# Six shared tiles behind the routed ones instead of five, and the first products of layer 1 moved ahead of the border between the phases

## What is computed

```
# layer 0
xn = layernorm(x)
x = x + attention(xn) + ffn0(xn)
# ffn0: softmax router, top 2 of 8 experts, and one shared expert for every token
#   expert(x) = silu((x @ w1 + b1) * (x @ w3 + b3)) @ w2 + b2          (256 -> 352 -> 256)
# layer 1
xn = layernorm(x)
z = sigmoid(xn @ Wz + bz);  h~ = xn @ Wh + bh
h_t = (1 - z_t) * h_(t-1) + z_t * h~_t;   attn1 = sigmoid(h @ Wg + bg) * h
# ffn1: s = sigmoid(xn @ gate.T); the better group of 4 experts, its top 2, weights normalised
#   lat = xn @ fc1.T; routed = sum_e weight_e * relu2(lat @ w1_e) @ w2_e; then @ fc2.T
#   shared = relu2(xn @ up.T) @ down.T
x = x + attn1 + ffn1(xn)
```

## Time and profile before

| | |
|---|---|
| runs | 1211.9, 1207.92, 1206.44 us |
| median | 1207.92 us |
| span of the profiled execution | 1206.9 us (the page gives no other time of it) |
| PE busy | 1111.1 us, 92% |
| DVE, ACT, POOL busy | 897.4, 676.1, 529.1 us |
| first product of the experts phase | 462.10 us |
| first product of layer 1 | 829.58 us |

### The profile page before, as it was taken

The page is one execution under the profiler, slowest core; times in us unless marked ns, Lnnn a source line. Parts: engine busy times, 40 slices in busy tenths (PEclk is TensorE's granted clock), DMA queues, the critical chain, the costliest instruction groups (busy, mean ns, idle before and its releaser), DMA issues. The chain is left out here.

```text
span 1206.9 us, 26712 instructions
## 1 busy us (share of the span) xinstructions
PE 1111.1 (92%) x8873; PEld 745.7 (62%) x8905; DVE 897.4 (74%) x2217; ACT 676.1 (56%) x1463; POOL 529.1 (44%) x743
## 2 busy tenths in 40 slices
PE   4789999999999987998999999996999999999998
PEld 2345555555455546887999888983656646546555
DVE  5778887888888757975766657775876877877876
ACT  2256565555556564565656656664654664664653
POOL 5443434334243235844444444423646547447414
PEclk9689999999999999999999999998999999999999
DMA  5538544354533404665232453452241331331211
GB/s 146 112 67 237 102 80 98 80 111 96 93 81 80 99 19 155 215 179 165 79 127 83 119 163 124 126 149 85 89 141 36 106 126 48 105 102 64 96 45 62
DMA packets 105044, 129.36 MB, mean 107 GB/s; under 512 B 14976, under 2 KB 92736, under 8 KB 103936
## 3 DMA queue, kind: packets, MB, share of 16 engines
q1 hardware_dynamic: 93952, 109.27, 33.8%
q0 software_dynamic: 6912, 18.88, 5.6%
q10 hardware_dynamic: 4096, 0.14, 0.2%
HBM read 84.70 MB, written 43.38 MB: 106 GB/s over the span
## 5 line engine op out<-in xcount | busy, mean ns | idle before, releaser
L537 ACT ACTIVATE p<-bank 128x384 f32<-128x384 f32 (+1 forms) x384 | 191.9, 530 | 186.4 <-PE bank L937 118.8
L757 DVE TENSOR_REDUCE neg_max<-bank 128x1 f16<-128x384 f32 (+3 forms) x352 | 219.7, 640 | 64.7 <-PE bank L925 56.4
L452 POOL TENSOR_SCALAR_AFFINE_SELECT p<-p 128x256 f32<-128x256 f32 x256 | 104.1, 410 | 247.3 <-ACT p L537 246.7
L922 PE MATMUL bank<-k_stack,q_stack 96*128 96x384 f16 (+3 forms) x512 | 133.5, 313 | 20.1 <-DVE neg_max L757 13.1
L1377 POOL DMA_INDIRECT fetched<-xn_dram,token_now x80 | 81.2, 1015 | 42.8 <-POOL token_now L1373 30.6
L937 PE MATMUL bank<-q_stack,k_stack 97*128 97x512 f16 (+1 forms) x256 | 91.5, 362 | 6.0 <-ACT p L537 3.5
L2006 POOL TENSOR_TENSOR up_lo<-up_sq,up_hi 128x512 f16<-128x512 f32 x32 | 43.9, 1399 | 120.7 <-ACT up_hi L2063 120.7
L2017 POOL TENSOR_TENSOR he_lo<-he_sq,he_hi 128x512 f16<-128x512 f32 x64 | 79.9, 1268 | 36.7 <-ACT he_hi L2106 36.6
L1461 ACT ACTIVATE a<-xbank,b 128x256 f32<-128x256 f32 (+1 forms) x126 | 58.6, 468 | 51.2 <-PE xbank L149 47.8
L1549 DVE TENSOR_TENSOR h_lo<-h,h_hi 128x256 f16<-128x256 f32 x159 | 68.4, 433 | 24.4 <-ACT h_hi L1470 23.5
L955 PE MATMUL bank<-p,v_aug 128*32 128x512 f32 (+3 forms) x1024 | 83.5, 445 | 0.8 <-DVE o_rows L737 0.8
(11 more groups left out here) (342 smaller groups left out, 3375.2 us busy)
## 6 DMA issues: line engine op xcount, KB each, us to landing
w_bc<-wT_dram SPq DMA_DIRECT2D x8, 2048.0 KB, 8.0
y_routed_dram<-y SPq DMA_DIRECT2D x37, 256.0 KB
w<-in_w SPq DMA_DIRECT2D x10, 704.0 KB, 6.9
pack<-in_pack SPq DMA_DIRECT2D x12, 342.0 KB, 4.1
xr<-in_x SPq DMA_DIRECT2D x8, 512.0 KB, 7.3
xn_dram<-xn SPq DMA_DIRECT2D x8, 512.0 KB, 3.1
qk_hi_dram<-qk_hi SPq DMA_DIRECT2D x16, 256.0 KB, 2.4
qk_lo_dram<-qk_lo SPq DMA_DIRECT2D x16, 256.0 KB, 2.4
```

Source lines behind the costliest of these rows:

```text
L452: pool.affine_select(out=diagonal, in_=diagonal, pattern=[[0, 2], [1, P]], compare_op=ALU.is_ge, fill=0.0, base=0, channel_multiplier=-1). ...
L537: act.activation(p32[:, s // GH % 2, s % GH, cols], s_bank[n][:, 0:cols.stop - cols.start], ACT.Exp).then_inc(p_exp.sem, 1)
L757: dve.tensor_reduce(neg_max[:, g % 2, 0:GH * TT].rearrange("p (h t) -> p h t", t=TT)[:, heads[0]:heads[-1] + 1, j], a_bank[c % 2][:, 0:len ...
L922: pe.matmul(to[:, at * w:(at + 1) * w], q_stack[0:STK, u, h0 + h, j * P:(j + 1) * P], k_stack[0:STK, u, h0 + h, 0:w], start=at == 0, stop= ...
```

## The change

The tail has six tiles and the head ten. The normalising of the first rows moves to stage 4, behind `hidden`; their turning stays in the last stage, now 5, as do the two halves, which leave the tail functions. `first_slots(1)` and `neg_bz` go to stage 4. In its tail PE appends `first_products`: `gate`, `lat` and `z0` of step 0; ACT makes the sigmoid and `lat_hi` there. Step 0 of layer 1 starts with the wait before `h0`. SP loads the three bias tensors in the prologue of the experts phase. The PSUM banks are declared once, and `l1_y` shares the memory of `turned`.

```diff
-TAIL_TILES = 5
+TAIL_TILES = 6
...
                 if stage not in (HEAD, TURN):
-                    if stage == 1:
-                        load_turned(HEAD_TILES + 3, HEAD_TILES + 4, i)
+                    if stage in range(1, TAIL_TILES - 3):
+                        load_turned(HEAD_TILES + 2 + stage, HEAD_TILES + 3 + stage, i)
...
# SP, prologue of the experts phase (were at the start of layer 1's block)
+                sp.dma_start(front.bias[:, :], w["bias"]).then_inc(front.loaded.sem, 16)
+                sp.dma_start(front.corr[:, :], w["corr"].partition_broadcast(P)).then_inc(front.loaded.sem, 16)
+                sp.dma_start(front.neg_bz[:, :], w["bias"][:, BZ:BZ + DC]).then_inc(front.loaded.sem, 16)
...
# ACT, tile
-                if stage == TAIL_TILES - 1:
-                    first_normalise()
                 for m in range(HM):
                     hidden(i, m)
+                if stage == TAIL_TILES - 2:
+                    first_normalise()
+                if stage == TAIL_TILES - 1:
+                    first_x_high()
...
             def tail(i, u):
+                act.wait_ge(front.lg_psum.sem, front.lg_psum.at(0))
+                act.activation(front.sc[:, :, :], bank[0][:, 0:TT * E].rearrange("p (t e) -> p t e", e=E),
+                               ACT.Sigmoid).then_inc(front.sc_s.sem, 1)
+                act.wait_ge(front.lat_psum.sem, front.lat_psum.at(0))
+                act.activation(front.lat_hi[:, :], bank[1][:, :], ACT.Copy).then_inc(front.lat_hi_s.sem, 1)
...
# DVE, tile
-                elif stage == TAIL_TILES - 3:
+                elif stage == TAIL_TILES - 4:
                     first_sums(0)
                     first_sums(1)
-                elif stage == TAIL_TILES - 2:
+                elif stage == TAIL_TILES - 3:
                     first_sums(2)
                     first_sums(3)
                     first_statistics()
+                elif stage == TAIL_TILES - 2:
+                    dve.wait_ge(front.loaded.sem, front.loaded.at(0))
+                    dve.tensor_scalar(front.neg_bz[:, :], front.neg_bz[:, :], -1.0, None, ALU.mult).then_inc(front.neg_bz_s.sem, 1)
+                    first_slots(1)
+                elif stage == TAIL_TILES - 1:
+                    first_x_low()
...
# PE
+            def tail(i, u):
+                out(i, u)
+                first_products(i)
+
+            def first_products(i):
+                pe.wait_ge(front.xT_lo_s.sem, front.xT_lo_s.at(0))
+                pe.wait_ge(prod_s.sem, prod_s.at(i))
...
+                for t in range(TT):
+                    tok = slice(t * P, (t + 1) * P)
+                    mm = three_products(pe, bank[0][:, t * E:(t + 1) * E], ...)
+                mm.then_inc(front.lg_psum.sem, 1)
+                from_x(bank[1][:, :], "fc1", LAT).then_inc(front.lat_psum.sem, 1)
+                from_x(bank[2][:, :], "wz", P).then_inc(front.z_psum.sem, 1)
...
# layer 1, PE's step (ACT's sigmoid and lat_hi likewise)
-                pe.wait_ge(xT_lo_s.sem, xT_lo_s.at(b))
                 if before:
+                    pe.wait_ge(xT_lo_s.sem, xT_lo_s.at(b))
                     pe.wait_ge(he_sq_s.sem, he_sq_s.at(b - 1))
...
+                    mm.then_inc(lg_psum.sem, 1)
+                    from_x(ring("lat")[:, :], "fc1", slice(0, LAT)).then_inc(lat_psum.sem, 1)
+                    from_x(ring("z0")[:, :], "wz", slice(0, P)).then_inc(z_psum.sem, 1)
                 pe.wait_ge(sc_s.sem, sc_s.at(b))
```

More of the change, by code:

```diff
@@ L102, in sb @@
             return ctx.enter_context(nc.sbuf_tensor(name, shape, dt))
+        self.bank = [ctx.enter_context(nc.psum_tensor(f"bank{i}", [P, 512], F32)) for i in range(8)]
         self.xr = sb("xr", [P, TT, D])
+        self.x1 = sb("x1", [P, TT, D])
         self.x_loaded = Signal(nc, ctx, "x_loaded", 16)
@@ L223, in mix_phase @@
         run = route["run"]
-        bank = [ps(f"bank{i}", [P, 512]) for i in range(8)]
+        bank = carried.bank
         w_loaded = sig("w_loaded", 16 * 8)
@@ L1114, in __init__ @@
         self.tile_out = sb("y", [P, ETOK // P, D])
+        self.bias = sb("l1_bias", [P, 3 * DC])
+        self.neg_bz = sb("neg_bz", [P, DC])
+        self.corr = sb("corr", [P, E])
+        self.sc = sb("l1_sc", [P, TT, E])
+        self.lat_hi = sb("lat_hi", [P, S], F16)
         self.slot_s = sig("slot_s", 2)
@@ L1126, in __init__ @@
         self.tile_stored = sig("y_stored", 16)
+        self.loaded = sig("l1_loaded", 16 * 3)
+        self.neg_bz_s = sig("neg_bz_s", 1)
+        self.lg_psum = sig("l1_lg_psum", 1)
+        self.lat_psum = sig("lat_psum", 1)
+        self.z_psum = sig("z_psum", DC)
+        self.sc_s = sig("sc_s", 1)
+        self.lat_hi_s = sig("lat_hi_s", 1)
 def experts_phase(nc, w, dram, consts, route, packed, front, carried):
@@ L1181, in experts_phase @@
         posf = sb("posf", [P, T // P, 2])
-        bank = [ctx.enter_context(nc.psum_tensor(f"xbank{i}", [P, 512], F32)) for i in range(8)]
+        bank = carried.bank
         front_bank = bank[6:8]
@@ L1501, in first_normalise, with first_x_high @@
                 ins.then_inc(front.xn_ready.sem, 1)
-            def tail(i, u):
+            def first_x_high():
                 for c in range(DC):
@@ L1636, in first_statistics, with first_x_low @@
                 ins.then_inc(front.dve_ln.sem, 2)
-            def tail(i, u):
+            def first_x_low():
                 for c in range(DC):
@@ L1642, in tail @@
                                       ALU.subtract).then_inc(front.xT_lo_s.sem, 1)
-                total_shared(i, TAIL_TILES - 1, (HEAD_TILES - 1) // 2)
-                first_slots(1)
+            def tail(i, u):
+                total_shared(i, HEAD_TILES + TAIL_TILES - 2)
             def done(n, ins):
@@ L1779, in after_first, with tail, from_x @@
                     pe.nop(nofuse=True)
-            over_experts(pe, lambda: None, new_expert, tile, after_first, lambda e, u, first: None, table, out)
+            def tail(i, u):
+                out(i, u)
[3 more added lines that the diff above has]
+                pe.wait_ge(prod_s.sem, prod_s.at(i))
+                def from_x(to, name, n):
+                    at, (_, width) = PACK[name]
+                    return three_products(pe, to, lambda c: pack_hi[:, at + c * width:at + c * width + n],
+                                          lambda c: pack_lo[:, at + c * width:at + c * width + n],
+                                          lambda c: front.xT_hi[:, c, :], lambda c: front.xT_lo[:, c, :], range(DC))
+                at = PACK["gate"][0]
+                for t in range(TT):
+                    tok = slice(t * P, (t + 1) * P)
+                    mm = three_products(pe, bank[0][:, t * E:(t + 1) * E], lambda c: front.xT_hi[:, c, tok],
+                                        lambda c: front.xT_lo[:, c, tok], lambda c: pack_hi[:, at + c * E:at + (c + 1) * E],
+                                        lambda c: pack_lo[:, at + c * E:at + (c + 1) * E], range(DC))
+                mm.then_inc(front.lg_psum.sem, 1)
+                from_x(bank[1][:, :], "fc1", LAT).then_inc(front.lat_psum.sem, 1)
+                from_x(bank[2][:, :], "wz", P).then_inc(front.z_psum.sem, 1)
+            over_experts(pe, lambda: None, new_expert, tile, after_first, lambda e, u, first: None, table, tail)
 PACK = {}
@@ L1816, in layer1_phase @@
         NU = UP // P
-        bias = sb("l1_bias", [P, 3 * DC])
-        neg_bz = sb("neg_bz", [P, DC])
-        corr = sb("corr", [P, E])
+        bias, neg_bz, corr, sc, lat_hi = front.bias, front.neg_bz, front.corr, front.sc, front.lat_hi
         minus_half, nothing, minus_mean, shift = front.minus_half, front.nothing, front.minus_mean, front.shift
@@ L1855, in layer1_phase @@
         comb_hi, comb_lo = (sb(f"comb_{k}", [P, S], F16) for k in ("hi", "lo"))
-        y = sb("l1_y", [P, TT, D])
-        bank = [ctx.enter_context(nc.psum_tensor(f"ybank{i}", [P, 512], F32)) for i in range(8)]
+        y = carried.turned[:, :, :, :, :].rearrange("p a b c n -> p (a b c n)").bitcast(F32)[:, 0:TT * D].rearrange("p (t d) -> p t d", t=TT)
+        bank = carried.bank
         out_bank, comb_bank = (bank[3], bank[4], bank[5], bank[7]), bank[6]
@@ L2022, in _ @@
         def _(act):
-            act.wait_ge(loaded.sem, loaded.at(0))
-            act.wait_ge(neg_bz_s.sem, 1)
+            act.wait_ge(front.neg_bz_s.sem, 1)
             def normalise(b, u):
@@ L2065, in step @@
             def step(b, u, before, more):
[L2066 to L2070, removed]
+                if before:
+                    act.wait_ge(lg_psum.sem, lg_psum.at(b))
+                    act.activation(sc[:, :, :], ring("gate")[:, 0:TT * E].rearrange("p (t e) -> p t e", e=E),
+                                   ACT.Sigmoid).then_inc(sc_s.sem, 1)
+                    act.wait_ge(lat_psum.sem, lat_psum.at(b))
+                    act.activation(lat_hi[:, :], ring("lat")[:, :], ACT.Copy).then_inc(lat_hi_s.sem, 1)
```

(10 more changed lines are left out.)

32 lines of the change are left out of this document (9 added, 23 removed).

## The result

The changed kernel takes 1211.83 us (median of 5 runs, 1210.75 to 1215.3) against 1207.14 us before in the same runs (1205.88 to 1211.9): a ratio of 1.0037 with a 95% interval of 1.0022 to 1.0052, or +4.5 us (2.7 to 6.3). The forecast was +5.0 us and 1212.9 us. The profiled execution took 1210.75 us, the fastest of its five, with a span of 1209.0, 2.1 more than the span before. That is why the spans differ by less than the medians.

A forecast was written before the change was run, and what follows sets the result against it. PE, busy 92% of the span, was taken to set the end, except at step 0, where the gathers do. Head -1.4, tail and border +2.4, clock +4.0 made +5.0 on 1207.92: 1212.9 us, range 1205 to 1217.5.

The forecast's parts named there:

- Head: Table after tile 7: PE idles 5.4 us for DVE's place(7), so one tile less saves only 1.4 us; clock 2.0.
- Tail: Last tiles before the border: the sixth tile fills the wait for the normalised rows and costs only +0.2 us.
- First products ahead of the border: Tail's end into step 0: gate, lat and z0 delay border and gathers; u3 2.4 us later, including the tail's +0.2.
- The gathers end the chain: Step 0 of layer 1: POOL's eighth gather ends last, so PE idles 5.3 us before u3.
- third rival: Step 0: gathers do not set it, PE's h0 starts 2.5 us earlier; sum -1.9, 1206.0 us; chance 0.10.
- Clock: Behind the waits before the table and before u3: half clock costs 2.0 us each, +4.0 for both.
- first rival: Both new waits of PE: the clock stays up; sum +1.0, 1208.9 us; chance 0.17.
- second rival: Both new waits of PE: clock stays low long after, 3.3 us each; sum +7.6, 1215.5 us; chance 0.22.

The follow-up runs named there:

- e5: The kernel before with only its table one tile earlier, waiting for prod of tile 7: 1213.76 us, ratio 1.0042 to the kernel before.
- e9: The changed kernel with the table's products reordered, the eight columns of place(7) multiplied last: 1204.4 us, ratio 0.9969 to the kernel before.
- e2: The changed kernel with gate, lat, z0 and ACT's sigmoid and lat_hi back behind the border: 1208.23 us, ratio 1.0016 to the kernel before.
- e8: The changed kernel with DVE's sums of step 0 put behind its first squares and scans: 1206.79 us, ratio 0.9990 to the kernel before.
- e12: e10 with gate, lat, z0 and the sigmoid back behind the border: 1201.59 us, ratio 0.9951 to the kernel before.
- e10: The changed kernel with the edits of e8 and e9 together: 1202.45 us, ratio 0.9948 to the kernel before.
- e4: The changed kernel with unread products filling PE's waits before the table and before u3: 1207.86 us, ratio 0.9999 to the kernel before.
- e1: The changed kernel with POOL's eight gathers issued ahead of the border instead of behind it: 1211.61 us, ratio 1.0032 to the kernel before.
- e11: The changed kernel with POOL waiting for ACT's early sigmoid, then one small memset before the border: 1216.86 us (2 runs), ratio 1.0076 to the kernel before.
- e3: The changed kernel with the last eight columns of in_column placed by POOL instead of DVE: 1209.17 us, ratio 1.0011 to the kernel before.

## Why the prediction was right

In the profiled pair the head gives +0.5 us, the routed tiles -1.1, tail and border up to u3 +1.45, the clock from u3 to g0 +1.3: together the 2.1 by which the spans differ. I take the -1.1 as no part of the change (the last statistics start at 815.73 instead of 816.31, and a wait of DVE for a stored `y`, 1.19 us in the trace of before, is not in the other), though no run isolates it; without it the trace gives +3.2, inside the interval of 2.7 to 6.3. By steps:

- **Head, -1.4 + 2.0 = +0.6 forecast.** +0.5 seen in this pair. The wait came as written (4.96 against 5.4 us, from DVE's last columns), and e5 and e9 show it from both sides: put in alone it costs 5 us, filled it gives 5.4 back. The table's half clock was 2.35, not 2.0, and it is no constant: behind waits of 4.9 to 5.1 us the table lost 1.2 (e5), 2.35 (after) and 2.7 us (e2).
- **Tail, +0.2.** The tile did fill the wait. DVE's sum was the last thing before `out(5)`, as forecast. With the statistics 0.58 us earlier in this execution, its start at 824.70 stands for 825.28, where I had 825.95; its end, 826.83, stands for 827.41 against `out(4)`'s 827.77. So the term was -0.4. Of the difference to my +0.2, 0.4 us arise already at DVE's first `prod` of stage 4, which starts 0.29 us behind the start of the last statistics (816.02 against 815.73); before it was 0.70 (817.01 against 816.31).
- **First products ahead of the border, +2.4 with the tail.** They end 3.2 us behind `out(5)`, the block opens 0.34 behind PE where I took 0.6, and u3 starts 1.45 us later than in the kernel before (845.15 + 0.58 less 844.28). So this step was about 1 us too high: 0.6 from the tail's term, the rest from the products and the opening. The mechanism is e2's: 2.1 per mille, 2.5 us, back when they are moved behind the border again (2.4 at g0 in its trace).
- **The gathers end the chain.** True by the chain of waits, and by e8: take DVE's sums out of the way and the wait before u3 is gone. The third rival priced PE's early start at 2.5 us; with the gathers off the path, e12 against e10 has 0.6 us of it at g0.
- **Clock, +4.0.** 2.35 + 1.28 = 3.6 in the trace of e4, 4.6 us by its ratio, within its uncertainty. In step 0 PE itself lost more: its wait before g0 shrank from 0.82 to 0.27 us, which gave 0.55 back. The first rival (clock stays up) had +1.0; the second needed 3.3 at each place. Neither was the case here. (Read off the low stretch is rather 6.8 us than 6.6, 821.2 to 828.1; half of it is 3.4.)
- **Forecast +5.0, measured +4.5.** The mechanisms were right as far as the runs show them; that the numbers lie only 0.5 us apart is in part luck. Taken from the traces, the terms come to 0.5 + 1.45 + 1.3 = 3.2 us, so the sum was some 1.8 us too high, 1.0 at the border and 0.7 in the clock of step 0, and the ratio with its interval of 2.7 to 6.3 can't tell 3.2 from 5.0.

The page "TensorE: Matmul & The Clock Gate" of the Trainium skill (section Terms) prices a throttled stretch by its length times the share of pulses withheld. The trace agrees once the length is counted only where PE works. The granted clock was low from 517.8 (0.89 in 517 to 518, 0.50 in 518 to 519) to 524.6 (0.69 in 524 to 525), 6.8 us. From 519.54, the table's first product, to 524.6 are 5.1 of them, of which half is 2.5, and 2.35 were lost. The 1.8 us before that, in which PE was idle, cost nothing, which is why the second rival's 3.3 was too much.

## What to carry to other kernels

A tile moved into a wait saves only what is not given back elsewhere: here the 6 us of the head went into a longer wait ahead of the table (4.96 us instead of 0.76) and a table at the half clock (2.35), and a later border (1.45 us in the trace) with the low clock behind u3 (1.3) came on top. Before moving work over a border, find what ends last behind it: moving one step of DVE, which stood between the gathers and PE, gave 5.7 us, where moving products back over the border (e2) gave 2.5 and moving gathers ahead of it (e1) nothing clear. Where a wait stays, let PE do in it what is ready, as 56 of the table's 64 column products in e9.

## What the runs showed of the hardware

- **Behind POOL's last instruction a block took long to end.** From there to the opening of the next block 8.2 us (e1, gathers) and 7.6 us (e11, a memset of 0.10 us) passed, in one trace each. In the kernels before and after nothing of it is seen: POOL ends near 818, and the next block opens past 829. In e11 a memset of 0.10 us late before the border brought g0 5.0 us later (34.18 against 29.20).
- **The clock may fall after PE is back at work.** In e2 the first five instructions of u3 ran at 0.38 us each and those after the sixth at 0.63, 1.3 us behind the end of the wait; in e10 it took four instructions, and the change came about 1 us behind it. In e3 the granted clock was 1.00 from 518 to 521 us, through the wait of 2.82, and 0.57 from 521 to 525, with the table under way from 521.09. And the length of the wait alone did not decide: 2.53 us left the clock up in e8 and e12, 2.54 us was followed by the half clock in e10, 2.82 us in e3.
